# First expert network of a four-layer stack: input split once, second layer from rounded products, combine weights at the input of the second layer

## The chip, the cores and the metric

The kernel runs on one core of a Trainium2 chip. The time is the device time of one execution in microseconds; lower is better. The engines are TensorE (PE in the profile; PEld is its weight load), VectorE (DVE), ScalarE (ACT), GpSimd (POOL) and SyncE (SP), which issues the transfers.

## What is computed

Four layers, each an attention and a feed-forward network with a residual, on 1024 tokens of 128 features. The change is in the network of the first layer, 8 experts of width 512, two per token:

```python
scores = xf @ Wg; w, idx = top_k(scores, 2); w = softmax(w)
xhat = (xf - mu) * rsqrt(var + EPS)
normed = xhat[None] * gamma[:, None] + beta[:, None]
h = relu(einsum('end,edf->enf', normed, W1) + b1[:, None])
out = einsum('enf,efd->end', h, W2) + b2[:, None] + xf[None]
y = einsum('ne,end->nd', cw, out)        # cw: the two weights of a token, else 0
```

All experts are computed for all tokens. Behind it come, in order, an attention of 16 heads with a gated network (layer 2), 16 experts of width 256 (the third network in this text), a pruned attention, 8 gated experts of width 512, and a last attention and network.

## The kernel before

Activations lie token-wise (`x`, `xn`, `att`: 128 tokens by 8 blocks by 128) or feature-wise (`xnT`, `kT`: 128 features by 1024 tokens). Feature-wise data come from TensorE transposes that ScalarE copies out of PSUM. A product that must be exact to more than one rounded pass is made by `split_products` (L1260): both operands are split into a rounded high part and a rounded low part (fp32r), and three products are summed, low by high, high by low, high by high. A plain `f32` product takes two passes, each a load and a matmul record in the profile.

The first expert network, `ffn0` (L454), runs in `ffn` on each engine, through `halves` (L540) with a loop over pairs of experts. One step is one half of the tokens (512) of one expert. TensorE (`ffn`, L1518) makes four hidden tiles of 128x512 in PSUM banks 0 to 3, three rounded products each, then the second layer of the step before, plain f32, token-wise: for 4 blocks of tokens and 4 tiles a product of 128x128, 32 passes. ScalarE (L1087) adds `b1` and takes the relu; VectorE (`combine`, L2276) multiplies the result by the combine weight of the token and adds it to `x`. `gamma` and `beta` differ per expert, so VectorE makes for every expert and half the scaled input in its high form, its full form and its low part (`scaled_input`, L2230, three instructions). GpSimd splits each expert's first weights (`split_weights`, L764: round, subtract); the second weights aren't split. The bias `b2` goes in with 16 small product passes ahead of the last output (`bias_products`, L1507).

The third network, `ffn1`, and the gated one, `ffn2`, run in `mixed` (L603 on the transfers' queue L595, GpSimd L781, ScalarE L1103, TensorE L1603, VectorE L2283). Their first steps are plain as above (`self.plain`). In the later ones the weights are applied to the hidden tiles: the combine weights are turned, stored to DRAM and loaded again as rows broadcast to all partitions (`cw_wide`, L615); VectorE computes (hidden + bias) x weight (`weigh`, L2292), ScalarE rounds it with a relu (`high_part`, L1117) and, for even tiles, writes the relu in full; the low part is made by VectorE for odd tiles and by GpSimd for even ones (L2308, L802). TensorE then makes the second layer feature-wise in three rounded products of 128x512 per tile, summed over all experts in two PSUM banks (`output`, L1683); at the end ScalarE copies the sums, TensorE turns them back (L1729), and VectorE adds them to `x` (`add_sums`, L2350).

The order on each engine is that of the program text; `pipelined` and `stages` (L55) interleave steps with a lag. Before the network stand, on VectorE, the norms (L2376 to L2387); on TensorE three transposes of halves (L1746 to L1748), and the fourth inside the first hidden tiles; on GpSimd the split of the first weights, then the reciprocal roots of the norms (`inverse_roots`, L698), then the next split. Behind the network ScalarE rounds the attention weights `wq1` and `wo1` in four instructions (`round_heads`, L1007), TensorE projects keys and values (L1753), turns the normed first half (L1757), and enters `wide_attention` (L1388), a loop of 32 steps (head by half). SyncE loads `wq1` and `wo1` (1 MB each) at the start (L645).

## Time and profile before

| | |
|---|---|
| median of 3 runs | 816.6 us (816.17 to 821.52) |
| profiled execution, its own time | 821.47 us |
| its span on the core | 819.8 us |
| mean granted TensorE clock | 0.927 of full |
| TensorE busy | 719.1 us, 4942 instructions |
| VectorE, ScalarE, GpSimd busy | 517.8, 439.8, 373.7 us |
| first expert network in the trace | about 88 to 198 us |

Times in the trace count from the start of the span. A row of the timeline gives start, duration and instruction with output and inputs by name; matmul durations overlap, so the pace is read from the distance of starts. The granted clock is in shares of 2.4 GHz; its lower level is 0.5.

### The profile page before, as it was taken

How to read it: one execution, taken by the hardware profiler on the slowest of the kernel's cores; microseconds unless marked ns; L12 is line 12 of the kernel's file. 1: busy time of each engine (PE TensorE's matmuls, PEld its weight loads, DVE VectorE, ACT ScalarE, POOL GpSimd, SP SyncE). 2: the span in 40 equal slices, each digit the busy share in tenths (PEclk: the TensorE clock that was granted, in tenths of full speed). 3: DMA queues.
4: the chain of work that ended last, by engine and by line, in shares of the span. 5: the costliest groups of instructions: out<-in, count | busy, mean ns of one | idle time of the engine just before them, and what ended most of it. 6: DMA issues, size and time to landing. Idle time of an engine off the chain costs nothing. (4 is left out here: it accounts for less than half of the span.)

```text
span 819.8 us, 14606 instructions
## 1 busy us (share of the span) xinstructions
PE 719.1 (88%) x4942; PEld 584.4 (71%) x4942; DVE 517.8 (63%) x1415; ACT 439.8 (54%) x1344; POOL 373.7 (46%) x375
## 2 busy tenths in 40 slices
PE   6986799999899999897679999788879999996775
PEld 3654699998688887775558788556658888884754
DVE  5797774445676666575646677758765566566554
ACT  3893334444577776563124777489734466653221
POOL 6663312112576644433112677485441488864001
PEclk9599799999999999998959999979989999998669
DMA  7000011110000000000003445000010322200000
GB/s 277 2 2 26 14 27 52 40 49 14 1 2 2 2 8 2 1 1 0 7 21 97 145 141 177 16 2 2 3 48 26 103 97 90 78 14 1 0 1 26
DMA packets 14277, 33.13 MB, mean 40 GB/s; under 512 B 1744, under 2 KB 5864, under 8 KB 13952
## 3 DMA queue, kind: packets, MB, share of 16 engines
q1 hardware_dynamic: 14208, 32.26, 12.0%
q8 instruction: 37, 0.61, 0.3%
q14 instruction: 32, 0.26, 0.1%
HBM read 31.63 MB, written 0.62 MB: 39 GB/s over the span
## 5 line engine op out<-in xcount | busy, mean ns | idle before, releaser
L1233 PE MATMUL banks<-input_hi,weights_in_lo 128*128 128x512 f32 x296 | 123.9, 418 | 18.4 <-PEq L1617 11.9
L1233 PE MATMUL banks<-input_lo,weights_in_hi 128*128 128x512 f32 x296 | 118.9, 402 | 0.0
L1233 PE MATMUL banks<-input_hi,weights_in_hi 128*128 128x512 f32 x296 | 118.6, 401 | 0.0
L1233 PEld LDWEIGHTS banks<-weights_out,hidden 128*128 128x128 f32 x864 | 105.6, 200 | 11.1 <-issue 8.1
L1233 PE MATMUL banks<-weights_out,hidden 128*128 128x128 f32 x864 | 106.9, 284 | 7.0 <-PEq L1561 6.3
L992 ACT ACTIVATE probabilities<-banks,neg_max 128x128 f32<-128x128 f32 x256 | 92.3, 479 | 17.5 <-DVE neg_max L1945 17.5
L1095 ACT ACTIVATE hidden<-banks,cols 128x512 f32<-128x512 f32 x80 | 54.1, 689 | 75.5 <-ACTq L1093 75.1
L703 POOL TENSOR_TENSOR rstd<-var_eps,neg_half 128x4 f32<-128x4 f32 x24 | 24.9, 1038 | 136.1 <-POOLq L702 115.2
L1233 PEld LDWEIGHTS banks<-input_hi,weights_in_lo 128*128 128x128 f32 x296 | 57.5, 194 | 32.4 <-issue 17.3
L992 ACT ACTIVATION_READ_ACCUMULATOR probabilities<-banks,neg_max 128x1 f32 x256 | 72.9, 319 | 0.0
L813 POOL TENSOR_TENSOR hidden<-hidden,scratch 128x512 f32<-128x512 f32 x48 | 62.0, 1291 | 19.4 <-ACT hidden L1114 16.8
L1233 PEld LDWEIGHTS banks<-input_hi,weights_in_hi 128*128 128x128 f32 x296 | 57.5, 194 | 12.8
L1114 ACT ACTIVATE hidden<-banks 128x512 f32<-128x512 f32 x64 | 38.2, 599 | 51.6 <-PE banks L1233 51.4
L1233 PEld LDWEIGHTS banks<-input_lo,weights_in_hi 128*128 128x128 f32 x296 | 57.7, 195 | 10.3
L2280 DVE SCALAR_TENSOR_TENSOR x_tok<-banks,combine_weights,x_tok 128x128 f32<-128x128 f32 x104 | 29.3, 344 | 52.9 <-DVEq L2254 38.7
L867 POOL TENSOR_TENSOR scratch<-values_state,self_weight 128x512 f32<-128x512 f32 x32 | 33.3, 1041 | 59.4 <-DVE self_weight L2088 59.4
L2298 DVE TENSOR_TENSOR banks<-banks,hidden 128x512 f32<-128x512 f32 x48 | 33.5, 698 | 32.9 <-POOL hidden L813 32.6
L787 POOL TENSOR_TENSOR weights_in_lo<-weights_in,weights_in_hi 128x256 fp32r<-128x256 f32 (+1 forms) x20 | 24.8, 1241 | 56.2 <-ACT weights_in_hi L1135 56.2
L2071 DVE TENSOR_REDUCE row_max<-banks 128x4 f32<-128x512 f32 x32 | 22.1, 691 | 44.8 <-PE banks L1426 44.8
L771 POOL TENSOR_SCALAR weights_in_hi<-weights_in 128x512 fp32r<-128x512 f32 (+2 forms) x13 | 20.9, 1604 | 61.4 <-POOLq L770 61.4
L1233 PE MATMUL banks<-hidden_hi,weights_out_lo 128*128 128x512 f32 x116 | 47.9, 413 | 0.0
L1233 PE MATMUL banks<-hidden_hi,weights_out_hi 128*128 128x512 f32 x116 | 46.2, 398 | 0.0
(277 smaller groups left out, 1734.3 us busy)
## 6 DMA issues: line engine op xcount, KB each, us to landing
scratch<-cw_rows SPq DMA_DIRECT2D x19, 512.0 KB, 3.9
weights_out<-w_in SPq DMA_DIRECT2D x17, 256.0 KB, 2.8
weights_in<-w_in SPq DMA_DIRECT2D x8, 512.0 KB, 3.6
weights_in<-w_in SPq DMA_DIRECT2D x9, 256.0 KB, 3.0
weights_in<-w_in SPq DMA_DIRECT2D x16, 128.0 KB, 2.2
weights_out<-w_in SPq DMA_DIRECT2D x16, 128.0 KB, 2.1
wq<-w1q_in SPq DMA_DIRECT2D x1, 1024.0 KB, 4.9
wo<-w1o_in SPq DMA_DIRECT2D x1, 1024.0 KB, 7.0
```

The lines of the kernel that those rows point to most:

```text
L703: pool.tensor_tensor(rstd[:, four], var_eps[:, four], neg_half[:, four], ALU.pow)\
L771: pool.tensor_scalar(w_hi[:, sub, n], w_in[:, n], 1.0, None, ALU.mult)\
L787: pool.tensor_tensor(w_lo[:, e % 2, n], w_in[:, n], w_hi[:, e % 2, n], ALU.subtract)\
L813: pool.tensor_tensor(h, h, cw_wide[:, e % 2, half * 512:(half + 1) * 512], ALU.mult)\
L867: pool.tensor_tensor(mva[:, n % 2, :, :], mv[:, four, :], self_w[:, n % 2, :, None].broadcast_to([P, 4, D]), ALU.mult)\
L992: act.activation(prob[:, n // 2 % 2, h, :], b8(n % (2 if prune else 3))[:, i, :], ACT.Exp, bias=neg_max8[:, n % 4, i:i + 1], accum_out=z[: ...
L1095: act.activation(hT[:, half, fc, :], bank[f.hidden_bank(n, fc)][:, :], f.first, **kw)\
L1114: act.activation(h_full[:, j, :], bank[f.hidden_bank(s, fc)][:, :], f.first, **kw)\
L1233: return pe.matmul(o, l, rh, start=start, stop=stop, **kw)
L2071: dve.tensor_reduce(m, b4(1 + n % 2), X_AX, ALU.max, negate=True).then_inc(st.sem, st.one())
L2280: dve.scalar_tensor_tensor(x[:, b, :], ps[:, t, :], cw[:, b, bass.ds(e, 1)], x[:, b, :], ALU.mult, ALU.add).then_inc(st.sem, st.one())
L2298: dve.tensor_tensor(up, up, h, ALU.mult).then_inc(weighted_ready, 1)
```

## The change

`ffn0` becomes an `Experts` with 4 plain steps and 12 later ones, and runs in `mixed`. What that does:

- The input is split once per half, without `gamma` and `beta`: ScalarE copies the transposed tokens as `in_hi` and `kT` (`enter_experts`), VectorE makes the low part. `scaled_input` is gone.
- `gamma` is multiplied into the first weights: ScalarE's or GpSimd's rounding takes it as a scale, and GpSimd multiplies the raw weights by it in an additional instruction ahead of the subtraction.
- `beta` times the first weights is added to `b1`: 32 one-column plain products into bank 3 (`shifts`), 20 behind the first transposes, 12 behind the last of those ahead of the network, and one addition on VectorE. For that all first weights are loaded into the places of `wq1` and `wo1`, whose own loads come after it.
- In steps 4 to 15 the second layer is feature-wise in three rounded products per tile, with the weights applied to the hidden tiles as in the third network. Both ends of the sum (copy, turn, add, then the norms of both halves) are those of `mixed`.
- `b2` goes in with `mixed`'s products. The rounding of `wq1` and `wo1` is taken apart: the first part before the sums, the other three in steps 2, 4 and 6 of the attention loop.

```diff
@@ class Experts
+        ffn0 = Experts(E0, F0, False, ACT.Relu, "b1_0", None, cw_rows0, 4, 2, "gamma0")
+                self.ring = 8 // self.FC
+                self.lag = self.ring // 2
+                self.shared = 4 // self.FC
@@ SyncE
-            sp.dma_start(wq1[:, :, :], w1q_in).then_inc(w1_attn_loaded, 16)
-            sp.dma_start(wo1[:, :, :], w1o_in).then_inc(w1_attn_loaded, 16)
-            load_experts(w0_in, ffn0)
+            for k in range(2):
+                sp.dma_start(w0_first[k], w0_in[4 * k:4 * k + 4, :, 0:F0].rearrange("e p n -> p e n"))\
+                    .then_inc(w0_first_loaded, 16)
+            def load_heads():
+                sp.wait_ge(shift_done, 1)
...
+            load_mixed(w0_in, ffn0, load_heads)
@@ GpSimd
+            def low_weights(lo, raw, hi, gamma):
+                if gamma is not None:
+                    pool.tensor_scalar(raw, raw, gamma, None, ALU.mult).then_inc(st.sem, st.one())
+                    pool.wait_ge(st.sem, st.n)
+                return pool.tensor_tensor(lo, raw, hi, ALU.subtract)
...
-            split_weights(ffn0, 0)
+            split_weights(ffn0, 0, col("gamma0", 0))
             inverse_roots((0, 0, 1, 1))
-            split_other_experts(ffn0)
+            mixed(ffn0)
@@ ScalarE
+            def enter_experts(half):
+                act.wait_ge(transposed, 1)
+                act.sem_inc(transposed, -1)
+                tokens, source = slice(half * 512, (half + 1) * 512), bank[6 - half][:, :]
+                act.activation(in_hi[:, 0, tokens], source, ACT.Copy).then_inc(st.sem, st.one())
+                act.activation(kT[:, tokens], source, ACT.Copy).then_inc(st.sem, st.one())
+                act.wait_ge(st.sem, st.n)
+                act.sem_inc(input_hi_ready, 1)
...
+                if f.gamma:
+                    act.wait_ge(shift_ready, 1)
...
                     if s % 2 == 0 and s // 2 > f.new_from:
                         round_second(s // 2)
                     if s % 2 == 1 and s // 2 + 2 < f.E:
                         round_first(s // 2 + 2)
-                    if f.gated:
+                    if f.FC == 4:
                         for fc in range(4):
                             high_part(s, fc)
@@ TensorE, in hidden() of mixed
+                        if f.gamma and (s, fc) == (0, 2):
+                            transpose_half(1, source, 5)
+                        if f.gamma and (s, fc) == (0, 3):
+                            pe.wait_ge(shift_ready, 1)
...
+                        elif not f.gated and s >= f.shared:
+                            before = s - f.shared
+                            if before < f.plain:
+                                pe.wait_ge(first_ready, f.first_count(before, fc))
+                            elif fc % 2 == 0:
+                                pe.wait_ge(weighted_ready, f.weighted_count(before, fc))
                             else:
+                                pe.wait_ge(lo_ready, f.lo_count(before, fc))
@@ TensorE
+            def shifts(first, last):
+                for k in range(first, last):
+                    e, fc = k // ffn0.FC, k % ffn0.FC
+                    m = mm(bank[3][:, k:k + 1], w0_first[e // 4][:, e % 4, fc * P:(fc + 1) * P], col("beta0", e))
+                return m
+            pe.wait_ge(w0_first_loaded, 32)
             transpose_half(0, xn, 4)
+            shifts(0, 20)
             transpose_half(0, att, 6)
             transpose_half(1, xn, 7)
-            ffn(ffn0, b2_0, None, w("r0"))
+            shifts(20, 32).then_inc(shift_done, 1)
+            mixed(ffn0, b2_0, att, w("r0"))
@@ VectorE
+                    elif f.FC == 4 and f.plain <= s < f.steps:
+                        for fc in range(3):
+                            weigh(s, fc)
+                        low_part(s, 1)
+                        weigh(s, 3)
+                        low_part(s, 3)
...
-            for half in range(2):
-                if half == 1:
-                    norm_apply(1, xn, att, norm_tok_ready)
-                dve.wait_ge(feat_ready_dve, 1)
-                dve.sem_inc(feat_ready_dve, -1)
-                scaled_input(0, 0, (half,))
+            split_input(0, kT)
+            norm_apply(1, xn, att, norm_tok_ready)
+            dve.wait_ge(shift_done, 1)
+            dve.tensor_tensor(b1_shifted[:, :], bank[3][:, 0:E0 * F0 // P], col("b1_0", 0, E0 * F0 // P), ALU.add)\
+                .then_inc(shift_ready, 1)
+            split_input(1, kT)
...
+            mixed(ffn0, [], add_inputs)
+            for half in range(2):
+                add_sums(half)
+                norm_stats(half, x, 1e-5)
             norm_apply(0, x, xn, norm_tok_ready)
-            norm_stats(1, x, 1e-5)
+            norm_apply(1, x, xn, norm_tok_ready)
             split_input(0)
-            norm_apply(1, x, xn, norm_tok_ready)
```

## Rows read from the trace of the kernel before

**Rows 1.** The page's part 1: busy us, share, instructions.

```profile
PE 719.1 (88%) x4942; PEld 584.4 (71%) x4942; DVE 517.8 (63%) x1415; ACT 439.8 (54%) x1344; POOL 373.7 (46%) x375
```

**Rows 2.** Window 103 to 205 us: PE, PEld, DVE, ACT, POOL busy (instructions), clock.

```profile
103.00:205.00 102.00, 101.26 (x705) 91.78 (x704) 52.62 (x151) 44.84 (x65) 18.31 (x13) 1.00 0.12 37
```

**Rows 3.** TensorE's timeline in the first expert network: start, us, instruction.

```profile
129.35 0.48 PE L1233 MATMUL banks<-input_hi,weights_in_lo 128*128 128x512 f32 x1
...
132.17 3.73 PE L1233 MATMUL banks<-weights_out,hidden 128*128 128x128 f32 x32
135.66 0.48 PE L1233 MATMUL banks<-input_hi,weights_in_lo 128*128 128x512 f32 x1
```

**Rows 4.** TensorE's timeline in the third network, two starts 17 steps apart.

```profile
467.46 0.39 PE L1233 MATMUL banks<-input_hi,weights_in_lo 128*128 128x512 f32 x1
...
514.84 0.39 PE L1233 MATMUL banks<-input_hi,weights_in_lo 128*128 128x512 f32 x1
```

**Rows 5.** Groups of lines by form, 470 to 515 us, the third network.

```profile
L806 POOL TENSOR_TENSOR hidden_lo<-hidden,hidden_hi 128x512 fp32r<-128x512 f32 x16 | 20.7, 1296 | 12.5 <-ACT hidden L1128 12.5
...
L2304 DVE SCALAR_TENSOR_TENSOR banks<-banks,cols,scratch 128x512 f32<-128x512 f32 x17 | 12.7, 749 | 0.0
...
L2315 DVE SCALAR_TENSOR_TENSOR hidden_lo<-banks,hidden_hi 128x512 fp32r<-128x512 f32 x16 | 10.9, 679 | 0.0
...
L1126 ACT ACTIVATE hidden_hi<-hidden 128x512 fp32r<-128x512 f32 x16 | 10.1, 634 | 11.4 <-DVE hidden L2304 11.4
L1123 ACT ACTIVATE hidden_hi<-banks 128x512 fp32r<-128x512 f32 x16 | 9.3, 582 | 0.0
```

**Rows 6.** GpSimd's timeline before the first expert network.

```profile
71.52 1.50 POOL L771 TENSOR_SCALAR weights_in_hi<-weights_in 128x512 fp32r<-128x512 f32 x1
...
75.29 1.04 POOL L703 TENSOR_TENSOR rstd<-var_eps,neg_half 128x4 f32<-128x4 f32 x1 [0.92 <-POOLq L702]
```

**Rows 7.** Two windows (clock); one-column products; their loads at low clock.

```profile
79.00:80.00 1.00, 0.00 (x0) 0.00 (x0) 0.71 (x3) 0.60 (x1) 0.53 (x1) 0.79 0.00 0
775.00:776.50 1.50, 1.50 (x12) 1.50 (x11) 0.68 (x2) 0.00 (x0) 0.00 (x0) 0.74 0.00 0
...
762.31 1.84 PE L1233 MATMUL banks<-cols,xn_feat 128*128 128x1 f32 x16
...
L1233 PEld LDWEIGHTS banks<-row_weights,xn_tok x2: 338/338/338, 775.8 to 776.0; 128*128 128x128 f32 x2
```

**Rows 8.** TensorE's timeline at the entry of the first expert network.

```profile
77.80 1.08 PE L1239 MATMUL banks<-identity,xn_tok 128*128 128x128 f32 x4
83.28 1.09 PE L1239 MATMUL banks<-identity,att_tok 128*128 128x128 f32 x4 [4.40 <-PEq L1237]
...
88.61 0.77 PE L1233 MATMUL banks<-input_hi,weights_in_lo 128*128 128x512 f32 x1 [2.87 <-PEq L1528]
...
95.11 0.47 PE L1233 MATMUL banks<-input_hi,weights_in_lo 128*128 128x512 f32 x1 [0.97 <-PEq L1528]
```

**Rows 9.** TensorE's timeline at the exits of the first and third network.

```profile
198.31 1.88 PE L1233 MATMUL banks<-ctx_feat,square_weights 128*128 128x512 f32 x4
...
201.65 0.63 PE L1239 MATMUL banks<-identity,xn_tok 128*128 128x128 f32 x4 [0.47 <-PEq L1237]
...
204.47 0.47 PE L1233 MATMUL banks<-input_hi,input_lo 128*128 128x512 f32 x1 [0.28 <-PEq L1393]
...
205.81 0.63 PE L1239 MATMUL banks<-identity,xn_tok 128*128 128x128 f32 x4 [0.41 <-PEq L1237]
...
520.43 0.60 PE L1729 MATMUL banks<-identity,att_tok 128*128 128x128 f32 x4
...
527.58 0.63 PE L1239 MATMUL banks<-identity,xn_tok 128*128 128x128 f32 x4 [2.15 <-PEq L1237]
```

**Rows 10.** ScalarE's rounding of attention weights; a window in the attention loop.

```profile
L1012 ACT ACTIVATE weights_in_hi<-wq x1: 1045/1045/1045, 190.8 to 190.8; 128x1024 fp32r<-128x1024 f32 x1
...
240.00:260.00 20.00, 20.00 (x168) 16.22 (x167) 12.89 (x49) 14.84 (x61) 13.28 (x12) 1.00 0.00 1
```

More of the change, by code:

```diff
@@ L550, in halves @@
             close()
-            if after_first:
-                after_first()
-            if iterations > 1:
-                with eng.Fori(1, iterations) as i:
-                    for stage, n, back in stages(order, groups, True, True):
-                        stage(i - back, n)
-                    close()
-            for stage, n, back in stages(order, groups, False, True):
-                if before_last and stage is last and n == groups - 1:
+            for stage, n, back in stages(order, 2, False, True):
+                if before_last and stage is last and n == 1:
                     before_last()
-                stage(iterations - 1, n)
+                stage(0, n)
             close()
@@ L827, in mixed @@
                     else:
-                        low_part(s)
+                        for fc in range(0, f.FC, 2):
+                            low_part(s, fc)
                     if s % 2 == 0 and e > f.new_from:
@@ L1100, in ffn, with mixed @@
                 order = [(hidden, range(4), 0)]
-                halves(act, order, f, st.close, {2: router_exp} if f.E > 1 else {})
-            def mixed(f):
-                tokens_in = enter_halves(f)
+                halves(act, order, st.close)
+            def mixed(f, tokens_in=None, before_sums=None):
+                tokens_in = tokens_in or enter_halves(f)
                 def first_layer(s, fc):
@@ L1191, in _ @@
             narrow_attention(False)
-            for dst, half, at, done in ((xnT, 0, 4, feat_ready), (kT, 0, 6, feat_ready_dve),
-                                        (xnT, 1, 7, feat_ready), (kT, 1, 5, feat_ready_dve)):
-                act.wait_ge(transposed, 1)
-                act.sem_inc(transposed, -1)
-                act.activation(dst[:, half * 512:(half + 1) * 512], bank[at][:, :], ACT.Copy).then_inc(done, 1)
-            ffn(ffn0, False)
-            round_heads()
+            take_router_tokens(0)
+            enter_experts(0)
+            take_router_tokens(1)
+            mixed(ffn0, enter_experts, round_first_queries)
             evacuate_context_keys()
@@ L1541, in hidden @@
                         m = split_products(bank[at_bank][:, :],
-                                           lambda part: f.w1((w_lo, w_hi)[part], sub, fc),
-                                           lambda part: (in_lo, in_hi)[part][:, at, tokens], True, True)
+                                           lambda part: f.w1((w_lo, w_hi)[part], 0, fc),
+                                           lambda part: (in_lo, in_hi)[part][:, 0, tokens], True, True)
                         if f.gated:
-                            if not begun and fc == 0:
+                            if half == 0 and fc == 0:
@@ L1723, in mixed @@
                         output(s - f.lag)
-                    if s == 3 and not f.gated:
+                    if s == f.turn_at and not f.gated:
                         turn_weights()
@@ L2273, in ffn @@
                     return
-                halves(dve, order, f, st.close, between, before_last)
+                halves(dve, order, st.close, between, before_last)
             def combine(e, n, ps):
@@ L2342, in mixed @@
                         weigh(s, 1)
-                    elif s == f.steps and not f.gated:
+                    elif s == f.steps and f.FC == 2:
                         low_part(s - 1, 1)
-                    if s == (1 if f.gated else 2):
+                    if s == f.turn_at - 1:
                         route(f.E, biases, [cw_ready], f.logits)
+                        if routed:
+                            routed()
                     if f.lag <= s < f.lag + f.plain:
```

294 lines of the change are left out of this document (107 added, 187 removed).

## The prediction

> **What bounds the kernel now.** I read the page first: TensorE is busy for 88% of the span, VectorE for 63% [rows 1]. Then the windows by stage: from 103 to 205 us, where the first expert network runs, TensorE is busy for 101.26 of 102.00 us at full clock, VectorE for half of it and GpSimd for 18% [rows 2]. So inside this network only TensorE's own work counts. The timeline of TensorE gives the step: 12 products of 128x512 from 129.35, 32 products of 128x128 from 132.17, the next step at 135.66 [rows 3]. That is 6.31 us a step (one half of the tokens, one expert), 2.82 in the first layer and 3.49 in the second, with no gap. At both ends of the network the chain is another one: norms on VectorE, transposes, copies on ScalarE, splits.
>
> **The second layer.** After the change 12 of 16 steps make the second layer from 12 rounded 128x512 products instead of 32 of 128x128. The third expert network already works so, with 6 and 6 products: 17 of its steps lie between 467.46 and 514.84 [rows 4], 2.787 us each, 0.2323 a product. Twenty-four products are 5.575 us, so a step saves 6.31 - 5.575 = 0.74 and the twelve save **8.9 us**. The four plain steps, the router and the turning of the weights stay as they are. The bias products have the same 1024 columns before and after: even. VectorE's inputs per expert and its combining go away, but they were beside TensorE: nothing.
>
> **New work of the other engines per step.** VectorE now weighs four tiles and makes two low parts: 4 x 0.75 + 2 x 0.68 = 4.4 us of 5.6. ScalarE has four high parts and two full copies at 0.58 to 0.63, and half of two roundings of weights [rows 5]: about 4.3 us. GpSimd has two low parts at 1.3 [rows 5] and half of a split of each kind, 1.3 for the second weights and 2.8 for the first with the additional multiply: about 4.6. None is above 5.6, so no engine becomes the bound by its sum. The order matters: in the steps where ScalarE rounds the next expert's first weights it waits for the last hidden tile of the step before it takes the first high part. Counted from the step's start: hidden tiles done at 2.9, rounding to 3.6, high 0 and full 0 to 4.9, high 1 to 5.4; VectorE has low 1 queued ahead of weigh 3, so low 1 to 6.1, weigh 3 to 6.8, high 3 to 7.4, low 3 to 8.1. TensorE's next step starts at 5.6 and wants the bank of tile 3 nine products later, at 7.65. That is a stall of 0.6 us. It can arise at steps 7, 9 and 11 (at step 5 the bias product of the next output gives 0.9 us of room; 13 and 15 round nothing): **+1.8**, between 0, if ScalarE's tiles run closer than their durations, and 12 x 0.6 = 7.2, if each step is so.
>
> **The entry.** Three things are added ahead of the first hidden product.
> First, GpSimd's split of the first weights gets a third instruction. The old first one takes 1.50, and the pair starts at 71.52 and is followed by the reciprocal root at 75.29 [rows 6]. With 1.50 + 1.50 + 1.27 the split ends at 75.9, and the root and the whole chain of norms behind it on GpSimd's queue come 0.6 later: **+0.6**, between 0 and 1.5.
> Second, 32 products with one column (the shift of the bias), each a load and a product in two passes. At full clock 16 passes take 1.84 us with the last one's end, 0.106 a pass; at the low clock two of the same loads start 0.21 apart [rows 7]. Twenty of them (40 passes) go between the transposes at 77.80 and those at 83.28 [rows 8], a hole from 78.7 on. The granted clock over 79 to 80 is 0.79 [rows 7], so it rose from 1.2 to 2.4 GHz at 79.4, after projections and transposes; with that the twenty end at about 83.6, 0.4 late. The other 12 (24 passes) stand alone on the path: 2.5 us at full clock, 5.1 at low. In the trace the clock fell again while such one-column products ran (0.74 over 775.0 to 776.5 [rows 7]), so I take the low clock: from 85.5 to 90.6, then the first hidden product, which was at 88.61 [rows 8].
> Third, what takes its place: VectorE's three instructions per half become one of 0.7, so the second half is ready sooner. From 90.6: six products at 0.43 (twice those of rows 3) to 93.2, transposes, two copies of 0.6 and one split: the second step's products at about 96.1, against 95.11 [rows 8]. **+1.0**; if the 12 run at full clock, -2.5 (92.6), and if all 32 run at the low clock, +4.6 (99.7).
> The new waits: SyncE waits for the end of the shift (about 90.6) with 2 MB of attention weights and, behind them, the third expert's weights; GpSimd's split of the second expert frees their place only at about 92, and they are wanted at about 107, the attention weights 90 us later: hidden, and a delay of 10 us would still be. ScalarE waits for VectorE's addition of the shift ahead of its first hidden tile, TensorE ahead of the fourth; the addition (0.2) is done before the first tile is: nothing, or 0.3 if VectorE's norm of the second half, queued ahead of it, is late.
>
> By the page "TensorE: Matmul & The Clock Gate" of the Trainium skill (section on LDWEIGHTS) a load takes its columns divided by 1.2, whatever the clock: 107 ns for 128 columns. The trace agrees at full clock (0.106) and not at the low one (0.21). An estimate by the page would take 24 passes at 2.6 us instead of 5.1 and put the entry 1.5 us before the old one; the rows decide here.
>
> **The exit.** Before, the residual was summed token-wise while TensorE ran: 3.34 us from the end of the outputs (198.31) to the transposes of the normed first half (201.65), and 2.82 more to the first query (204.47) [rows 9]. After, sums must be copied, transposed and added, and the norms of both halves follow one another. The third network ends so already: from the first transposes of the sums (520.43) to the transposes of the normed half (527.58) are 7.15 us [rows 9], which puts the query at 9.97 instead of 6.16, 3.8 later. Against it, the second norm now runs before the split, so that the pause at 205.81 (0.41, and what waits behind it) goes: I take back 0.6, **+3.2**, between 1.3 (the transposes alone) and 3.8.
> TensorE has about 3 us of nothing in that stretch, where before it had none. If its clock falls there, the projections, transposes and the first query, some 2.3 us, take twice as long; I take **+1.0**, between 0 and 2.3.
>
> **Roundings moved into the attention.** Four ScalarE instructions of 1.045 us [rows 10] ran under the end of the network. One still does; three go into steps 2, 4 and 6 of the attention loop. ScalarE is busy for 14.84 of 20.00 us there [rows 10], some 1.2 us free in a step of 4.7, while TensorE is full. A rounding just about fits: **+0.4**, between 0 and 3.1 (none fits).
>
> **The sum**, against the profiled execution: 821.47 (span 819.8) - 8.9 + 1.8 + 0.6 + 1.0 + 3.2 + 1.0 + 0.4 = 820.6, that is -0.9. The median of the runs shown is 816.6, 4.9 below the profiled one, so I forecast **815.7 us**.
>
> **Rivals.**
> (a) The shift runs at full clock. For it: a rise was just granted at 79.4. Against it: the fall beside one-column products [rows 7]. Entry -2.5 instead of +1.0: 812.2.
> (b) The order costs nothing: ScalarE keeps ahead, no stall, and exit and entry come out as their low ends allow. For it: the third network runs 17 steps without a gap [rows 4]. Against it: its high parts don't stand behind a rounding of the same step. -8.9 + 0.6 + 1.0 - 1.0 (half of the shift at full clock) + 0 = -8.3: 808.3.
> (c) The other side: the one-column products hold the path at the low clock, all 32 of them. 64 passes of 0.213 are 13.6 us, of which the hole before 83.28 hides 4.6. Entry +4.6 instead of +1.0 puts the sum at +2.7: 819.3. It decides from an entry 0.9 us later than forecast on, a second step's first product after 97.6 on this trace's scale. For it: up to 79.4 the clock was the low one; against it: it did rise there [rows 7].
> (d) The change doesn't deliver its step: every step of the twelve stalls on its low parts, not three. 7.2 instead of 1.8: 821.1. Against it: in other steps ScalarE takes high 0 from 1.7 us on.
>
> **How the numbers follow.** Forecast 0.46, (a) 0.18, (b) 0.14, (c) 0.16, (d) 0.06. 1% is 8.2 us, about what a measurement of this kernel tells from no change (three runs spread over 5.4 us). Faster by over 1% means below 808.4: half of (b) and the tails of (a), 0.12. Slower by over 1% means above 824.8: (c) or (d) with the high ends of exit and attention, 0.07. Within: 0.81. The range for 8 in 10 cuts half of (b) and the upper part of (c) and (d): 808.8 to 821.0. The forecast's own range is 813 to 818.5.
>
> **What would show it.** Right: steps of 5.58 us in the network's second part, with short gaps ahead of the fourth hidden tile in three of them; load durations of 338 ns, not 192, on the one-column products; the first query some 10 us after the sums' first transposes. Wrong: a step of 5.9 or more throughout (d); the second step's products before 94 (a) or after 97.6 (c); an attention loop whose first steps are longer by over 1 us.

## The result, and the profile after

The changed kernel takes 823.83 us (median of 19 runs, 819.82 to 828.72) against 816.83 of the kernel before in the same comparison (19 runs, 815.45 to 821.55). The ratio is 1.0078, with a 95% interval of 1.0058 to 1.0097. It is slower by 0.8%. The forecast was 815.7 with a range up to 821.0, so the forecast and its range are both wrong. Two single runs far from all others, one of 1045 us (before_pad8) and one of 3679 us (exit_fix), are left out of the medians further down. The profiled execution of the changed kernel is one of 824.99 us (span 823.0), 3.5 above the profiled one of before.

The page's part 1, against [rows 1] (busy us, share of the span, instructions):

```profile
PE 726.6 (88%) x4762; PEld 581.5 (71%) x4762; DVE 522.6 (64%) x1386; ACT 459.2 (56%) x1386; POOL 415.8 (51%) x407
```

TensorE has 180 instructions fewer and is busy for 7.5 us more. Fewer instructions with more busy time are a first hint at the clock (products of other widths have a part in it too). The same window as in [rows 2], with the columns PE, PEld, DVE, ACT and POOL busy, then the granted clock:

```profile
103.00:205.00 102.00, 96.92 (x469) 76.69 (x467) 65.80 (x138) 60.55 (x103) 59.89 (x45) 0.98 0.20 68
```

GpSimd went from 18 to 60 us of 102, and the window no longer has the full clock throughout. Then TensorE's timeline at the entry, against [rows 8]. The 32 `cols` products are the first 16 one-column products of two passes each:

```profile
74.52 2.07 PE L1264 MATMUL banks<-square_weights,att_feat 128*128 128x128 f32 x8 [2.96 <-DVE att_feat L1970]
76.60 1.09 PE L1270 MATMUL banks<-identity,xn_tok 128*128 128x128 f32 x4
77.48 3.87 PE L1264 MATMUL banks<-cols,wq 128*128 128x1 f32 x32
81.21 1.70 PE L1264 MATMUL banks<-cols,wo 128*128 128x1 f32 x8
...
84.51 5.12 PE L1264 MATMUL banks<-cols,wo 128*128 128x1 f32 x24
89.49 0.77 PE L1264 MATMUL banks<-input_hi,weights_in_lo 128*128 128x512 f32 x1
...
95.49 0.47 PE L1264 MATMUL banks<-input_hi,weights_in_lo 128*128 128x512 f32 x1
```

The last 12 products take 5.12 us at the low clock, as the prediction had it (85.5 to 90.6 there). The other twenty met both levels: the profile has the low clock up to 78.0 us, the full one up to 81.4, then the low one. From the first transposes to the second step it is 18.89 us, against 17.31 in before. What TensorE waited for between 97 and 200 us (in total, times, longest), a view that is empty for before:

```profile
PE banks L1264 <- POOL weights_out_lo L809: 1.2, 3, 0.4
PE banks L1264 <- DVE hidden_lo L2270: 0.6, 2, 0.3
```

And the steps, by the first product of each. A wait of 0.35 shows in the row, but the step that holds it is 6.21 us long (143.13 to 149.34), where its neighbour took 5.53:

```profile
137.60 0.40 PE L1264 MATMUL banks<-input_hi,weights_in_lo 128*128 128x512 f32 x1
...
143.13 0.39 PE L1264 MATMUL banks<-input_hi,weights_in_lo 128*128 128x512 f32 x1
...
145.72 0.51 PE L1264 MATMUL banks<-input_hi,weights_in_lo 128*128 128x512 f32 x1 [0.35 <-DVE hidden_lo L2270]
149.34 0.40 PE L1264 MATMUL banks<-input_hi,weights_in_lo 128*128 128x512 f32 x1
```

The exit, against [rows 9], has 9.98 us from the sums' transposes to the first query, and two windows show that the clock fell there (third last number), which it didn't in before:

```profile
192.96 0.60 PE L1712 MATMUL banks<-identity,att_tok 128*128 128x128 f32 x4
...
194.30 1.88 PE L1264 MATMUL banks<-ctx_feat,square_weights 128*128 128x512 f32 x4
...
200.10 0.63 PE L1270 MATMUL banks<-identity,xn_tok 128*128 128x128 f32 x4 [3.03 <-PEq L1268]
...
202.94 1.42 PE L1264 MATMUL banks<-input_hi,input_lo 128*128 128x512 f32 x1
```

```profile
200.00:201.00 1.00, 0.90 (x8) 0.93 (x9) 0.84 (x4) 0.15 (x1) 0.00 (x0) 0.93 0.00 0
201.00:204.00 3.00, 3.00 (x9) 1.94 (x9) 2.19 (x6) 0.98 (x3) 0.00 (x0) 0.50 0.00 0
```

From the first transposes (77.80 before, 76.60 after) to the first query (204.47, 202.94) the two profiles need 126.67 and 126.34 us. So in the stretch that the change touches nothing is lost in this pair. The 3.5 us arise later, in code that is the same in both. Two landmarks of TensorE there are the transposes of the third network's sums and the turning of the last gated network's weights. They lie 109.3 us apart before (520.43, 629.71) and 114.5 after (519.75, 634.24). The last row of before, then the two of after:

```profile
629.71 1.03 PE L1658 MATMUL banks<-identity,combine_weights 128*8 128x128 f32 x8
```

```profile
519.75 0.60 PE L1712 MATMUL banks<-identity,att_tok 128*128 128x128 f32 x4
...
634.24 0.93 PE L1641 MATMUL banks<-identity,combine_weights 128*8 128x128 f32 x7
```

The windows of this stretch, before and then after:

```profile
540.00:550.00 10.00, 9.53 (x95) 6.36 (x92) 6.02 (x10) 10.00 (x54) 6.79 (x13) 0.82 0.01 2
...
610.00:620.00 10.00, 7.05 (x40) 6.00 (x38) 5.68 (x9) 3.48 (x6) 2.35 (x1) 1.00 0.17 55
```

```profile
540.00:550.00 10.00, 10.00 (x67) 6.95 (x66) 4.90 (x7) 7.99 (x42) 6.60 (x12) 0.50 0.00 0
...
610.00:620.00 10.00, 7.05 (x23) 5.50 (x22) 5.05 (x10) 2.93 (x6) 4.06 (x2) 0.69 0.17 52
```

The code of this stretch is the same in both kernels. What differs in the rows is the clock: 0.50 instead of 0.82, and 0.69 instead of 1.00.

### The profile page after: what moved, and what is told of

Read it like the earlier page. It is cut to its first block and busy times, and to the rows that moved or that the text cites. A ratio compares the mean times of both kernels' runs of the same rounds, so it can differ in the third digit from the quotient of the medians.

```text
span 823.0 us, 14052 instructions
## 1 busy us (share of the span) xinstructions
PE 726.6 (88%) x4762; PEld 581.5 (71%) x4762; DVE 522.6 (64%) x1386; ACT 459.2 (56%) x1386; POOL 415.8 (51%) x407
## 5 line engine op out<-in xcount | busy, mean ns | idle before, releaser
L1000 ACT ACTIVATE probabilities<-banks,neg_max 128x128 f32<-128x128 f32 x256 | 90.5, 427 | 14.3 <-DVE neg_max L1937 14.1
L819 POOL TENSOR_TENSOR hidden_lo<-hidden,hidden_hi 128x512 fp32r<-128x512 f32 x50 | 64.6, 1295 | 43.1 <-ACT hidden L1154 40.7
L776 POOL TENSOR_TENSOR weights_in_lo<-weights_in,weights_in_hi 128x256 fp32r<-128x256 f32 (+2 forms) x33 | 42.5, 1287 | 60.3 <-ACT weights_in_hi L1165 59.2
L1264 PE MATMUL banks<-hidden_hi,weights_out_lo 128*128 128x512 f32 x164 | 67.6, 412 | 1.2 <-POOL weights_out_lo L809 1.2
L1264 PE MATMUL banks<-weights_out,hidden 128*128 128x128 f32 x480 | 61.3, 288 | 7.0 <-PEq L1559 6.3
L1000 ACT ACTIVATION_READ_ACCUMULATOR probabilities<-banks,neg_max 128x1 f32 x256 | 67.3, 267 | 0.0
L1264 PEld LDWEIGHTS banks<-weights_out,hidden 128*128 128x128 f32 x480 | 60.2, 204 | 9.8 <-issue 7.8
L1264 PEld LDWEIGHTS banks<-input_lo,weights_in_hi 128*128 128x128 f32 x296 | 58.3, 197 | 10.8
L1264 PE MATMUL banks<-hidden_hi,weights_out_hi 128*128 128x512 f32 x164 | 65.2, 398 | 0.0
L1264 PE MATMUL banks<-hidden_lo,weights_out_hi 128*128 128x512 f32 x164 | 49.2, 397 | 0.0
L2270 DVE SCALAR_TENSOR_TENSOR hidden_lo<-banks,hidden_hi 128x512 fp32r<-128x512 f32 x50 | 34.3, 686 | 22.6 <-ACT hidden_hi L1149 22.6
```

The source lines that it names most:

```text
L776: return pool.tensor_tensor(lo, raw, hi, ALU.subtract)
L819: pool.tensor_tensor(h_lo[:, j, :], h_full[:, j, :], h_hi32[:, j, :], ALU.subtract)\
L1000: act.activation(prob[:, n // 2 % 2, h, :], b8(n % (2 if prune else 3))[:, i, :], ACT.Exp, bias=neg_max8[:, n % 4, i:i + 1], accum_out=z[: ...
L1264: return pe.matmul(o, l, rh, start=start, stop=stop, **kw)
L2270: dve.scalar_tensor_tensor(h_lo[:, j, :], bank[f.hidden_bank(s, fc)][:, :], 0.0, h_hi32[:, j, :], ALU.max, ALU.subtract).then_inc(lo_ready, 1)
```

## The experiments

Two theories stood against each other. **Place against the clock:** the clock changes at moments that the program does not set, and the change moved the later stages to where more of their work falls under the low clock. **Own work:** the changed kernel does something more. Medians of one group of runs are compared with before's of the same group, which lies between 817.8 and 818.9 us; "+5.2" stands for 5.2 us above it.

**rep_before, rep_after.** Both kernels as they are, to have the mean granted clock of every run.

> The kernel before, unchanged, to have the granted clock of each of its runs. Time at the low clock is 2 x (1 - mean granted clock) x span: 119.7 us in its profiled run of 821.47 us. Theory (the clock): its ordinary runs of 816 to 817 us have 8 to 14 us less at the low clock, near 107 us, and the time of a run goes up by some 0.35 us per us at the low clock, as it does over the 19 runs of the changed kernel (116 us at 819.8 to 820.7 us, 130 us at 824.8 to 825.0). Rival (more work in the changed kernel): the ordinary runs have about 116 us at the low clock too, so at the same clock the changed kernel takes 4 us more.

> The changed kernel, unchanged, for a second profile and more runs. Theory (the clock): median 821 to 825 us; the stretch of 97 to 190 us has no low clock, and the runs differ only in stretches that the change doesn't touch (the entries of the pruned attention at about 535 to 552 us and of the last gated network at 595 to 621 us). Rival: where this profile is a fast run (820 us), those stretches look as in the first profile, and the saving is in the first network.

Before took 817.79 us, 0.9994 (0.9979 to 1.0009) of its own other runs at 818.85; after took 824.02 (+5.2), ratio 1.0065 (1.0037 to 1.0093). Time at the low clock, 2 x (1 - mean clock) x span, is 115.2 us in the mean of 47 runs of before (mean time 818.4) and 127.1 in 31 of after (823.6). Inside the changed kernel it sorts the runs: 113 to 119 us in those of 819.7 to 820.7, 128 to 133 in those of 824.8 to 825.8. A common straight line through the runs of before, after and the next two kernels gives 0.29 us per us at the low clock, and at an equal low clock after is 1.8 us above before. So of 5.2 us some 3.4 go with the clock (12 x 0.29) and 1.8 don't. That is a correlation over runs; it doesn't say what makes the changed kernel's runs have more of the low clock. Before's median run had 114 us and not 107: the theory's figure was off, its direction right.

The second profile of before (817.6 us) corrected a number. Its first transposes come at 75.41 and not at 77.80, with the same code; its clock rose at 31 us and not at 38. The execution on which the forecast's chain was worked out had been at the upper end of before's runs. Measured against the second profile, after is 1.2 us late at the first transposes. Other pairs of like rise say the same: 74.88 in before_pad3 against 76.08 in combined2 (29 us), 77.80 in before against 79.14 in exit2 (38 and 39 us). The Trainium skill, "TensorE: Matmul & The Clock Gate", Part 1, says that the window over which the gate of the clock watches TensorE runs freely and isn't reset when a kernel starts; the rises at 31 and 38 us in one and the same code agree.

**no_shift, order_fix.**

```diff
@@ no_shift: TensorE; VectorE copies b1 instead of adding
-            shifts(0, 20)
-            shifts(20, 32).then_inc(shift_done, 1)
+            pe.sem_inc(shift_done, 1)
@@ order_fix: ScalarE, odd steps; GpSimd, even steps
-round_first(e + 2); high_part(s, 0..3)
+high_part(s, 0..3); round_first(e + 2)
-low_part(s, 0); low_part(s, 2); split_second(e)
+split_second(e); low_part(s, 0); low_part(s, 2)
```

> Leaves out the 32 one-column products (beta is left out, b1 is used as it is); the loads into the places of wq1 and wo1 stay. Prediction's sum: the products cost about 8 us of TensorE on the path to the first hidden tile at the low clock, less what VectorE's norms hide: the first hidden tile comes at 83 to 86 us instead of 89.49, the whole 3 to 5 us earlier than the changed kernel. Theory (the clock): the first network starts earlier by that, but the median follows by it only as far as the low-clock time stays the same; anything from -8 to 0 against the changed kernel. Rival (the one-column products keep the engine busy and so the clock is regained sooner): less than 2 us saved.

> Two moves within the steps of the first network: ScalarE rounds the next first weights behind the step's high parts, GpSimd makes the low part of the second weights ahead of the step's low parts. Prediction's term of +1.8 us (three steps of 0.6 us) and the three waits for weights_out_lo of 0.4 us each that the first profile shows: 2.0 us less from the first network's start to the keys' projection behind it (104.8 us in the changed kernel). Theory (the clock): the median moves by that or by more in either direction, with the low-clock time of its runs. Rival: the waits return as others (weights in w_in later), under 0.5 us.

no_shift (it leaves `beta` out): 816.56 us (-2.3), 7.5 below rep_after; the first hidden tile comes at 85.85, 3.6 us earlier. order_fix: 818.47 us (-0.4), 5.5 below. From the second hidden step to the sums' transposes it needs 94.3 us; before needed 103.2 to the end of its outputs, after 97.0 and 97.5 in its two profiles. Its four steps from 142.75 to 164.93 us are of 5.55 us each, and the waits for low parts and for the low second weights are gone:

```profile
142.75 0.39 PE L1268 MATMUL banks<-input_hi,weights_in_lo 128*128 128x512 f32 x1
...
164.93 0.39 PE L1268 MATMUL banks<-input_hi,weights_in_lo 128*128 128x512 f32 x1
```

Both medians fell by about twice what the landmarks moved.

**before_pad3, before_pad8, after_pad5, after_pad12.** In the third network, where TensorE runs densely, n products are repeated:

```diff
+if f is ffn1 and (s, fc) == (10, 0):
+    for _ in range(n):
+        mm(bank[f.hidden_bank(s, fc)][:, :], f.w1(w_lo, sub, fc), in_hi[:, 0, tokens])
```

> The kernel before with three more products of 128x512 in the third network, where TensorE runs densely (0.2323 us each, 0.70 us in all; their result is overwritten). Theory (place against the clock): the stretch from the sums of the third network to the turned weights of the last gated network takes 109.3 us in both profiles of before, 114.5 in both of the changed kernel, 112.0 without the one-column products and 111.4 with the steps reordered, all with the same code; what differs is where it stands against the moments at which the clock changes. 0.70 us later it stands in before where it stands in the changed kernel: 114 us for the stretch, and the median rises by 3 to 6 us, not by 0.7. Rival (something of the changed kernel's own slows the stretch): 109.3 us, the median 0.7 us above before.

> The same with eight products, 1.86 us of work. Theory (place against the clock): the stretch stands where that of the reordered kernel stands, 111 to 112 us; the median 2 to 4.5 us above before, and less than 1 us above the one with three products, or below it. Rival: stretch 109.3 us, the median 1.9 us above before, 1.2 us above three products.

> The changed kernel with five more products of 128x512 at the same place (1.16 us of work). Theory (place against the clock): the stretch takes 111 to 112 us instead of 114.5, and the median falls by 1 to 3 us although work was added. Rival (something of the changed kernel's own slows the stretch): 114.5 us, the median 1.2 us higher, 825.1 us.

> The changed kernel with twelve more products (2.79 us of work). Theory (place against the clock): it stands as before's does, 109 to 110 us for the stretch, and the median is 820.5 to 823 us, below the changed kernel's 824.0 in spite of the work. Rival: 114.5 us, the median 826.8 us.

| | median us | before beside it | stretch expected | stretch in its profile |
|---|---|---|---|---|
| before_pad3 | 817.30 | 817.84 | 114 | 114.6 |
| before_pad8 | 818.32 | 817.84 | 111 to 112 | 112.4 |
| after_pad5 | 825.90 | 817.84 | 111 to 112 | 112.3 |
| after_pad12 | 824.18 | 817.84 | 109 to 110 | 109.9 |

The stretch came out within 0.6 us of what was expected, four times of four. The kernel before can show the "changed" 114.6 us, and the changed kernel, with 2.79 us more work, 109.9, near before's 109.3. The windows of before_pad3, to be read against the two pairs above:

```profile
540.00:550.00 10.00, 10.00 (x79) 6.61 (x77) 4.61 (x7) 8.48 (x43) 5.58 (x8) 0.50 0.00 0
...
610.00:620.00 10.00, 7.03 (x20) 5.47 (x19) 4.52 (x7) 2.54 (x5) 2.50 (x2) 0.66 0.17 53
```

and those of after_pad12:

```profile
540.00:550.00 10.00, 9.31 (x78) 6.07 (x74) 6.12 (x9) 9.33 (x52) 6.63 (x13) 0.72 0.00 1
...
610.00:620.00 10.00, 7.15 (x34) 5.76 (x33) 6.48 (x12) 4.08 (x7) 4.62 (x2) 1.00 0.17 52
```

The pads alone don't prove the push: the profiled execution of before_pad3 was the slowest of its twelve (823.29), and its clock first rose at 28.7 us, not at 31 or 38, so it was shifted against the clock by more than its pad. What shows the place is the time from the sums' transposes to the clock's next fall, over all eighteen profiles of this text. With 8.8 to 8.9 us the stretch takes 114.5 to 114.6 (after, rep_after, before_pad3), with 9.5 and 9.8 it takes 109.3 and 109.9 (rep_before, after_pad12), with 13.4 and 13.6 it takes 112.3 and 112.4 (after_pad5, before_pad8). Like places give like times, whichever the kernel.

So this stretch's 5 us are no property of the changed kernel. But the medians did not do what I expected of them. before_pad3 (-0.5) and before_pad8 (+0.5) did not rise by 2 us or more, and after_pad5 (+8.1) did not fall; after_pad12 (+6.3) got some of its work for nothing, but did not fall either. A median is over executions whose stages stand differently, and a shift of all of them only exchanges which are hit. The theory explains the pair of profiles; it does not by itself explain the medians.

**exit_fix, no_mult, early_shift, combined.**

```diff
@@ exit_fix: VectorE
-add_sums(0); norm_stats(0); add_sums(1); norm_stats(1); norm_apply(0); norm_apply(1)
+add_sums(0); norm_stats(0); add_sums(1); norm_apply(0); norm_stats(1); norm_apply(1)
@@ no_mult: GpSimd, low_weights
-                    pool.tensor_scalar(raw, raw, gamma, None, ALU.mult).then_inc(st.sem, st.one())
@@ early_shift: TensorE
+            shifts(0, 12)
             attention_output(False, w("wo0"), 1, 5)
             transpose_half(0, xn, 4)
-            shifts(0, 20)
+            shifts(12, 32).then_inc(shift_done, 1)
             transpose_half(0, att, 6)
             transpose_half(1, xn, 7)
-            shifts(20, 32).then_inc(shift_done, 1)
```

> VectorE applies the norm to the first half before it takes the statistics of the second. Prediction's exit term (+3.2 us and +1.0 us for a fall of the clock in the gap; both profiles of the changed kernel show 8.63 us from the keys' projection behind the network to the first query, against 6.16 in before, and a fall at 201 us): the first query comes 1.6 us earlier. Theory (place against the clock): if the shorter gap no longer lets the clock fall, 2 to 2.5 us earlier; the median 1 to 5 us below the changed kernel. Rival (the gap is hidden by the projections of values): under 0.3 us.

> Leaves out GpSimd's additional multiplication of the raw first weights by gamma in the low part (the low part is then that of the unscaled weights). Theory (contention): VectorE's var_eps instruction, 0.17 us in before and 1.25 us in the changed kernel, where GpSimd's instruction is still running beside it, takes 0.17 us again, and the transposes of the normed first half start 1.2 us earlier, at 75.4 us instead of 76.6 in a run of the same clock pattern; the three waits for the low second weights (1.2 us) in the first network go too. Prediction's figure for the first of these was 0.6 us, for the second nothing. Rival (the multiplication only fills idle time of GpSimd): no landmark moves.

> The same 32 one-column products, 12 of them in TensorE's idle time before the last output projection of the first attention (2.96 us of waiting for VectorE's att_feat), 20 behind the first transposes, none behind the last. Prediction's term (12 of them at the low clock on the path, 5.1 us in both profiles of the changed kernel): from the first transposes to the first hidden tile 9.5 us instead of 12.89, as without the products. Theory (place against the clock): the second hidden step no longer stands at a fixed distance behind the clock's rise (1.4 us in four profiles of five of the changed kernel), and the median falls by 3 to 7 us, more than the products' own time. Rival: the products delay the output projection by what they cost, and less than 1.5 us is won.

> The three moves together: early products, reordered steps, reordered exit. By the sum of the single ones from the changed kernel: 3.4 us (entry) + 2.8 us (steps, as measured with the reordered kernel) + 1.6 us (exit) = 7.8 us, so 816.2 us if the clock falls as often as in the changed kernel; theory (place against the clock): 811 to 816 us, faster than before. Rival (waits return elsewhere): 817 us or more, no better than before.

Before beside them: 817.80 us.

*exit_fix*, 824.18 us without its one far run (+6.4; 825.29 with it), missed: 9.46 us from the keys' projection to the first query instead of 8.63. The transposes came earlier, but the query's low part stood behind the second half's norm on VectorE.

*no_mult*, 824.10 us (+6.3): the landmark moved as expected (first transposes at 74.8 instead of 76.6 us; part of that is the clock, for exit_fix with a rise at 29 us like no_mult's has 76.3), the time did not. VectorE's timeline in the changed kernel, and then in no_mult:

```profile
72.46 1.25 DVE L1847 TENSOR_SCALAR var_eps<-mean_var 128x4 f32<-128x4 f32 x1
...
74.18 0.29 DVE L1970 TENSOR_TENSOR att_feat<-att_unscaled,banks 128x128 f32<-128x128 f32 x1
```

```profile
71.90 0.17 DVE L1844 TENSOR_SCALAR var_eps<-mean_var 128x4 f32<-128x4 f32 x1
...
72.54 0.29 DVE L1967 TENSOR_TENSOR att_feat<-att_unscaled,banks 128x128 f32<-128x128 f32 x1
```

and GpSimd's in the changed kernel at that time:

```profile
70.77 1.56 POOL L774 TENSOR_SCALAR weights_in<-weights_in,cols 128x512 f32<-128x512 f32 x1
72.42 1.26 POOL L776 TENSOR_TENSOR weights_in_lo<-weights_in,weights_in_hi 128x512 fp32r<-128x512 f32 x1
```

The instruction on 128x4 elements takes 1.25 us and ends at 73.71, GpSimd's subtraction at 73.68. In before the subtraction was over (74.37) when var_eps began:

```profile
73.10 1.27 POOL L774 TENSOR_TENSOR weights_in_lo<-weights_in,weights_in_hi 128x512 fp32r<-128x512 f32 x1
...
74.89 0.17 DVE L1855 TENSOR_SCALAR var_eps<-mean_var 128x4 f32<-128x4 f32 x1
```

So var_eps, and with it att_feat, for which TensorE waits, end 1.1 us late. How much of the 1.2 us that is isn't told by no_mult: it also frees GpSimd's own queue, which the third instruction keeps busy until 73.68 and on which the reciprocal root of the norms stands next. The Trainium skill, "GPSIMD Engine Reference", section Specifications, says that GpSimd shares its SBUF interfaces with VectorE, with contention when VectorE's instruction is in a 2-port mode or has two SBUF inputs. These rows fit it, though the profile doesn't name the mode of var_eps, and give the price. In the network the three waits for the low second weights are gone, but those for VectorE's low parts rose from 0.6 to 1.3 us; of 1.8 us in all 1.3 are left:

```profile
PE banks L1261 <- DVE hidden_lo L2267: 1.3, 4, 0.4
```

The entry of no_mult was 16.0 us long from the first transposes to the first hidden tile, not 12.9. All nine profiles with this entry have the one figure or the other: 12.8 to 12.9 in five (after, rep_after, after_pad12, order_fix, and filled below), 16.0 in four (after_pad5, exit_fix, no_mult, and exit2 below). To the second step it is 18.8 to 18.9 us in the five and 21.7 to 22.0 in the four. Before has 10.8, and 17.3 to the second step, in all four. exit2's rows show the second kind, the first twenty products taking 8.4 us instead of 5.3:

```profile
80.02 6.82 PE L1264 MATMUL banks<-cols,wq 128*128 128x1 f32 x32
86.71 1.84 PE L1264 MATMUL banks<-cols,wo 128*128 128x1 f32 x8
...
95.13 0.77 PE L1264 MATMUL banks<-input_hi,weights_in_lo 128*128 128x512 f32 x1
```

```profile
78.00:82.00 4.00, 4.00 (x20) 3.73 (x19) 3.49 (x16) 0.60 (x1) 1.01 (x1) 0.50 0.25 96
82.00:86.00 4.00, 4.00 (x20) 4.00 (x21) 3.26 (x17) 0.00 (x0) 1.01 (x1) 0.50 0.00 0
```

All at the low clock, that is the rival (c), whose mark was 19.8 us to the second step (97.6 less 77.80), in four executions of nine.

*early_shift*, 821.13 us (+3.3, against +5.2). Twelve products took 2.84 us in the idle time at the full clock. The other twenty met the low clock in this profile, and the first hidden tile came 12.6 us behind the transposes, not 9.5. With the same entry order_early and combined2 have 12.6 too, and combined alone the expected 9.5. (The 1.4 us in its expectation is a slip of mine: the second hidden step of those four profiles stands 0.3 to 0.5 us behind the clock's rise.) *combined*, 818.17 us (+0.4), ratio 1.0015 (0.9996 to 1.0033), no better than before; it has the exit of exit_fix (9.46 us).

**filled, exit2, order_early, combined2.**

```diff
@@ filled: TensorE, ahead of attention_output(False, w("wo0"), 1, 5)
+            for _ in range(10):
+                mm(bank[3][:, :], in_hi[:, 0, 0:P], in_hi[:, 0, 0:512])
@@ exit2: VectorE
+add_sums(0); norm_stats(0); add_sums(1); norm_apply(0); norm_stats(1); split_input(0); norm_apply(1)
```

> The changed kernel with ten more products of 128x512 (0.23 us each at the full clock; their result is overwritten) in the 2.96 us in which TensorE waits for VectorE's att_feat ahead of the last output projection. Theory (the entry's price is the clock's): the clock falls later, the 20 one-column products behind the first transposes take 4.7 us (12 of them took 2.84 us at the full clock in the early_shift kernel) instead of 5.3 or 8.4, and from the first transposes to the first hidden tile it is 10 to 12.5 us instead of 12.9 or 16.0; the median falls by 2 to 4 us though work was added. Rival (the clock falls during the one-column products whatever stands ahead of them): 12.9 or 16.0 us again, the median unchanged or up to 1 us higher.

> As exit_fix, and the low part of the first half's input ahead of the norm of the second half on VectorE. exit_fix took 9.46 us from the keys' projection to the first query, against 8.63: its transposes came 1.5 us earlier, but the first query then waited for the low part behind the second half's norm. With the low part moved: 7.0 to 7.3 us, 1.5 us less than the changed kernel; the median 1 to 3 us below 824. Rival (the query then waits for the loaded or rounded wq1): 8.6 us.

> order_fix and early_shift together, the exit as in the changed kernel. By the medians of the two (818.5 and 821.1, from 824.0) 815.6 us; by the clock's place anything from 813 to 818. Against combined (818.2, with the exit that cost 0.8 us): 0.8 us less or more. Faster than before's 817.8 by up to 2 us, if the moves add up.

> order_fix, early_shift and exit2 together: 1.5 us below order_early, 814 us; faster than before. Rival (place against the clock eats it): 816 to 819 us, no different from before.

Before beside them: 818.63 us. *filled*: 821.33 us (+2.7) with ten products more. The clock fell at 80 us, while the one-column products ran, so for the landmark the rival holds (12.77 us). Its median, 2.5 us better against before than the changed kernel's, is as the theory had it; which stage gained it is not shown. *exit2*: 820.75 (+2.1); 7.23 us to the first query as expected, and the clock does not fall in the gap. *order_early*: 819.30 (+0.7), 3.7 above the sum of its parts, with runs from 813.4 to 823.1. *combined2*: **813.16 us, ratio 0.9941 (0.9918 to 0.9964)**, faster than both kernels. Its exit:

```profile
188.97 0.60 PE L1716 MATMUL banks<-identity,att_tok 128*128 128x128 f32 x4
...
194.73 0.63 PE L1274 MATMUL banks<-identity,xn_tok 128*128 128x128 f32 x4 [1.64 <-PEq L1272]
...
197.55 0.47 PE L1268 MATMUL banks<-input_hi,input_lo 128*128 128x512 f32 x1 [0.28 <-PEq L1428]
```

8.58 us instead of 9.98, and from the first transposes (76.08) to this query 121.5 instead of 126.3. That is 4.9 of the 11 us between the medians of combined2 and the changed kernel. In the profiles another 5 lie in unchanged code, from this query to the third network's sums (311.9 against 316.8), and combined2's runs have 112 us at the low clock in the mean, the changed kernel's 127: by the line above 4.3 us of the 11 go with the clock.

## Why the prediction was wrong, step by step

| term | forecast | measured | from |
|---|---|---|---|
| second layer, 12 steps | -8.9 | -8.9 | order_fix: 94.3 against 103.2 |
| stalls | +1.8 | +2.7 to +3.2 | after 97.0, 97.5 against 94.3 |
| third GpSimd instruction | +0.6 | +1.2 | 76.6 against 75.4, no_mult |
| one-column products | +1.0 | +1.6 or +4.7 | 18.9 or 22.0 against 17.3 |
| exit with the clock's fall | +4.2 | +3.8, and +0.4 behind the query | 9.98 against 6.16; first query to the gated network's transposes 165.5 in after, 165.1 in exit2, which has no fall there |
| roundings in the attention | +0.4 | +0.2 | the same stretch, 165.1 in exit2 and combined2 against 164.8 |
| sum | -0.9 | +1.0 to +4.6 | |

**What bounds the kernel** held: TensorE's own work counts, and a step of the new form takes 5.55 us (forecast 5.575).

**The stalls** have the mechanism that was forecast (the step's fourth hidden tile, behind ScalarE's rounding), but in the changed kernel only the first of the three full ones shows, the step from 143.13. Three other steps of 6.2 us wait for what the prediction put at nothing: GpSimd makes the low second weights behind the step's low parts and, in the steps before, behind a split of three instructions. I had added GpSimd's work up (4.6 of 5.6 us) and followed only ScalarE's order. In no_mult, where those waits are gone, the three forecast ones stand (steps of 6.20, 6.08 and 6.06 us from 144.30, 156.14 and 167.89), so the one kind hides the other. Two moves in the order take away the whole 3 us.

**The third instruction** was charged with what follows it on its own queue (0.6). That is there: GpSimd is busy until 73.68, and in rep_before the reciprocal root started at 72.91. But it also overlaps an instruction of VectorE that then takes 1.25 us instead of 0.17, and the two delays run side by side; the shares of the 1.2 us are not shown.

**The one-column products** are the term that failed most, by 1.9 us in the mean. Mechanism, place and both prices were right, 12 at the low clock and all 32 at it (+4.6 forecast, +4.7 measured). The mistake was to take one profile's rise of the clock at 79.4 [rows 7] as given for every execution, and to call the other case a rival with a chance of 0.16. It is no other outcome of the change but a part of its executions. The mean over the nine profiles is +2.9.

**The page's rule** on loads: the Trainium skill, "TensorE: Matmul & The Clock Gate", section on LDWEIGHTS, gives a load its columns divided by 1.2 and names no clock: 107 ns for 128 columns. The 24 passes, each a load and a product, took 5.12 us at the low clock, 0.213 each, and 2.84 us, 0.118 each, at the full clock in early_shift. The trace decides against it here: a pass follows the clock.

**The exit** was read off the third network, and 7.14 + 2.84 us repeat its 7.15 + 2.82 [rows 9]. The two smaller terms were both wrong and nearly cancel: the 0.6 taken back did not come, and the clock's fall, put at 1.0, cost nothing up to the query and 0.4 behind it. That the sum is near is partly luck.

**Slips in the prediction's own sums.** Its timetable of a step gives a stall of 0.45 us (8.1 less 7.65), not 0.6; three would be 1.4. Its 0.43 us for a product at the low clock is what the trace shows, but not twice that of rows 3, which is 0.47. Rival (b) leaves out the exit's low end of 1.3 us; with it (b) is 809.6, not 808.3.

**The sum in the touched stretch** was then wrong by 2 to 5.5 us, in the mean of the nine entries (2.9) by some 3.5: about +2.6 instead of -0.9. With it I would have forecast 819. **The rest**, some 2.5 of 5.2 us, is put down to code that is not changed, for which the prediction had nothing. The eighteen profiles show that a single stage there moves by 5 us with its place against the clock and without any cause in its code. Why the changed kernel's executions are hit more often than before's (127 against 115 us at the low clock) stays open. One thing is seen in the profiles but was not tested alone: in before's four the second hidden step comes 0.5, 1.4, 2.0 and 2.0 us behind the clock's rise, in eight of the nine with the changed entry 0.3 to 1.0 us. TensorE's work ahead of it is now long enough to run until the clock rises, so the later stages would stand in the same place against the clock in many executions, a bad one, where before's are spread. That is argued, not shown.

**The range** had every term's bounds and none for stages behind the change. The three runs shown spread over 5.4 us, and the profiled one was at their upper end. That spread is the clock's, and the range should have carried it.

## What to carry to other kernels

Where one kernel's executions spread by more than the change is worth, take two profiles before a landmark is believed, and read the clock in the stages that the change doesn't touch. One-column products cost twice as much at the low clock, and in these traces it fell while they ran; put them where the engine idles at the full clock. When a step is added for several engines, write out the order on each queue, not only the sums: here two reordered pairs, the reordered exit and the early products took the median from 824.0 to 813.2 us, and 4.9 us of that can be seen in the stretch that they touch.

## What was not expected of the hardware

- The same unchanged stretch takes from 109.3 to 114.6 us over eighteen profiles, and like places against the clock's next fall give like times in both kernels.
- The clock fell at 80.2 us in filled while one-column products ran; TensorE had been busy without a gap from 76.0 us on.
- A VectorE instruction on 128x4 elements took 1.25 us beside a GpSimd subtraction on 128x512, and ended 0.03 us after it.
- 2.8 us of work added in the third network put the changed kernel only 1.2 us further above before (+6.3 against +5.2).
